# A gated cross-attention and ternary FFN layer: value products of 66 columns, square sums from bf16 parts, and another order of the steady slot

## The reference

```
h  = layernorm(x)
q  = rms_norm(h @ Wq + bq) * nq ;  k = rms_norm(ctx @ Wk + bk) * nk ;  v = ctx @ Wv + bv
a  = softmax(q k^T / sqrt(32)) v          16 heads of 32, within each tile of 128
x1 = x + tanh(g0) * (a @ Wo + bo)
u  = relu(layernorm(x1) @ T(Wfc))^2       T: ternary weights, hidden size 2048
out = x1 + tanh(g1) * rms_norm(u) @ T(Wproj)
```

## Time and profile before

| | us |
|---|---|
| median of 3 runs | 944.68 |
| lowest, highest | 942.75, 948.52 |
| span of the profiled execution | 945.4 |
| TensorE busy in it | 894.8 |
| ScalarE busy | 775.4 |
| VectorE busy | 715.2 |
| GpSimd busy | 572.2 |

### The profile page before, as it was taken

One profiled execution on the slowest core, in us unless ns is written; L12 is line 12 of the kernel. 1 busy time (PEld: TensorE's weight loads), 2 busy tenths in 40 slices (PEclk: granted clock), 3 DMA queues, 4 the chain that ended last, 5 costly groups with the idle time before them and its releaser, 6 DMA issues. The chain is left out here.

```text
span 945.4 us, 22870 instructions
## 1 busy us (share of the span) xinstructions
PE 894.8 (95%) x7958; PEld 535.9 (57%) x7958; DVE 715.2 (76%) x1448; ACT 775.4 (82%) x1559; POOL 572.2 (61%) x616
## 2 busy tenths in 40 slices
PE   5677798999999999999999999999999999999998
PEld 2333455466656656656656655556566656556664
DVE  6999999888877778878877778778777778776301
ACT  6888888888888888888888887888888888888673
POOL 1341436657676665657676665757676665757664
PEclk9797999999999999999999999999999999999999
DMA  9558874666666567666667665656765576755300
GB/s 360 141 96 206 201 157 79 113 112 124 120 128 118 110 121 124 123 118 119 120 127 127 100 122 112 122 115 126 121 135 112 105 128 117 127 91 97 68 24 34
DMA packets 319747, 115.80 MB, mean 122 GB/s; under 512 B 305168, under 2 KB 305168, under 8 KB 318096
## 3 DMA queue, kind: packets, MB, share of 16 engines
q1 hardware_dynamic: 319632, 114.34, 61.0%
HBM read 30.67 MB, written 8.39 MB: 41 GB/s over the span
## 5 line engine op out<-in xcount | busy, mean ns | idle before, releaser
L537 PE MATMUL up_pair<-ft,w 128*128 128x256 f16 x960 | 214.5, 273 | 0.2 <-DMA ft<-x_rows 0.2
L538 PE MATMUL up_pair<-ft,w 128*128 128x256 f16 x960 | 214.5, 273 | 0.0
L996 ACT ACTIVATE score_ps<-score_ps,exp_bias,exp_scale 128x128 f32<-128x128 f32 x512 | 189.9, 468 | 4.5 <-DVE exp_bias L1494 4.3
L2025 POOL TENSOR_TENSOR hh_sum<-hh_sum,hh_sb 128x512 f32<-128x512 f32 x112 | 159.1, 1421 | 49.5 <-ACT hh_sb L954 45.2
L552 PE MATMUL mix_ps<-w,big 128*128 128x512 bf16 x448 | 170.0, 380 | 0.7 <-DVE pt L1525 0.7
L553 PE MATMUL mix_ps<-w,big 128*128 128x512 bf16 x448 | 169.8, 379 | 0.0
L2015 POOL TENSOR_TENSOR big<-h_sb,big 128x512 f16<-128x512 f32 x128 | 149.4, 1167 | 25.1 <-POOL big L2015 9.1
L1970 POOL TENSOR_TENSOR ln_rstd<-ln_in,minus_half 128x1 f32<-128x1 f32 x64 | 36.9, 577 | 175.2 <-issue 145.2
L1327 DVE TENSOR_TENSOR p_rows<-score_ps,p_rows 128x512 f16<-128x512 f32 x128 | 85.5, 686 | 50.3 <-ACT p_rows L878 49.5
L878 ACT ACTIVATE p_rows<-score_ps 128x512 f16<-128x512 f32 x128 | 76.0, 639 | 40.1 <-DMA pt<-p_rows 39.8
L927 ACT ACTIVATE h_sb<-up_pair,relu_scale 128x512 f32<-128x512 f32 x120 | 81.7, 681 | 30.1 <-PE up_pair L538 29.8
(11 more groups left out here) (215 smaller groups left out, 2179.1 us busy)
## 6 DMA issues: line engine op xcount, KB each, us to landing
x_sb<-in_x SPq DMA_DIRECT2D x32, 256.0 KB, 3.1
ctx_sb<-in_ctx_t SPq DMA_DIRECT2D x32, 256.0 KB, 4.2
out<-out_sb SPq DMA_DIRECT2D x32, 256.0 KB, 2.3
big<-in_w_fc_t SPq DMA_DIRECT2D x4, 1024.0 KB, 5.3
big<-in_w_proj_t SPq DMA_DIRECT2D x4, 1024.0 KB, 5.9
pt<-p_rows SPq DMA_TRANSPOSE x128, 3.2
big<-in_wq_t SPq DMA_DIRECT2D x1, 1024.0 KB, 4.9
big<-in_wk_t SPq DMA_DIRECT2D x1, 1024.0 KB, 7.1
```

The source lines that it names most:

```text
L537: nc.tensor.matmul(dst[:, half], w, ft[i][:, c, :], start=(c == 0), stop=False)
L538: last = nc.tensor.matmul(dst[:, half], w, ft[i][:, C + c, :], start=False, stop=(c == C - 1))
L996: last = nc.scalar.activation(rows, rows, ACT.Exp, scale=exp_scale[:, :], bias=exp_bias[:, 4 * b + u:4 * b + u + 1])
L2025: nc.gpsimd.tensor_tensor(hh_sum[:, :], hh_sum[:, :], hh_sb[f % 2][:, :], ALU.add).then_inc(hsum_ready, 1)
```

## The change

1. *Values.* v_hi and v_lo of a head lie side by side in one tile, `v_both`. `wide_values` makes per head one 66-column product of p_hi with both, and one 33-column product of p_lo with v_hi: 32 products per slot in place of 48. The low part stands in columns of its own, so ScalarE copies it to SBUF (`values_low`, twice per slot), and VectorE's `wide_attention` adds it and then multiplies with the reciprocal, in place in SBUF. The results need four banks: b = 2 and 3 go to score banks 0 and 1, so `wide_values` waits there for k_raw and q_raw of the next tile, and the next `scores` for both halves of the attention.
2. *Square sums.* `hidden_split` on VectorE makes three bf16 parts of hh_sum (two copies, two subtractions, 128 x 256 each), and `square_sums_split` sums them with six bf16 products.
3. *Order.* The slots of all five queues are reordered. On SP, load_context moves from behind load_x to ahead of the last transpose of p, whose order becomes 0, 1, 2, 3, and the store goes to the end.

The first six slots and the closing slot keep their code, but for the shared tiles and one wait. The declarations of semaphores and of `ones_b`, and one memset, are left out here.

```diff
--- before.py
+++ after.py
@@ -63,14 +63,19 @@
             return [sem(f"{name}{i}") for i in range(n)]
 
 
-        score_ps = [stack.enter_context(nc.psum_tensor(f"score_ps{i}", [P, 512], F32)) for i in range(4)]
+        score_pair = stack.enter_context(nc.psum_tensor("score_pair", [P, 1024], F32))
+        score_ps = [score_pair[:, 0:512], score_pair[:, 512:1024]]
+        score_ps += [stack.enter_context(nc.psum_tensor(f"score_ps{i}", [P, 512], F32)) for i in (2, 3)]
         k_ps, q_ps, v_ps = score_ps[0:3]
         up_pair = stack.enter_context(nc.psum_tensor("up_pair", [P, 1024], F32))
         up_ps, up_b = up_pair[:, 0:512], up_pair[:, 512:1024]
-        mix_ps, tr_a = (stack.enter_context(nc.psum_tensor(n, [P, 512], F32)) for n in ("mix_ps", "tr_a"))
+        mix_pair = stack.enter_context(nc.psum_tensor("mix_pair", [P, 1024], F32))
+        mix_ps, tr_a = mix_pair[:, 0:512], mix_pair[:, 512:1024]
         o_ps = tr_a
         fc_ps = mix_ps[:, 512 - 8 * NU:512]
         pv_ps = [bank[:, 0:8 * (HD + 1)].rearrange("p (b u d) -> p b u d", b=2, d=HD + 1) for bank in (mix_ps, tr_a)]
+        wide_ps = [pair[:, :].rearrange("p (b k) -> p b k", b=2)[:, :, 0:8 * (HD + 1)].rearrange("p b (u c) -> p b u c", u=4)
+                   for pair in (mix_pair, score_pair)]
 
 
         ident = sb("ident", [P, P])
...
         warm_rows = w_hi[0][:, 0, 0:384]
-        v_hi = sb("v_hi", [P, H, HD + 1], F16)
-        v_lo = sb("v_lo", [P, H, HD + 1], F16)
+        v_both = sb("v_both", [P, H, 2 * (HD + 1)], F16)
+        v_hi, v_lo = v_both[:, :, 0:HD + 1], v_both[:, :, HD + 1:2 * (HD + 1)]
         p_inv = sb("p_inv", [P, H])
         p_rows = [sb(f"p_rows{i}", [P, 2, 512], F16) for i in range(PR)]
...
         t_scale = [out_sb[0][:, :].bitcast(BF16), sb("t_scale1", [P, 1024], BF16), out_sb[1][:, :].bitcast(BF16)]
+        pv_lo = t_scale[1][:, :].bitcast(F32).rearrange("p (i b u d) -> p i b u d", i=2, b=2, u=4)
+        hh_parts = abs_w[0][:, 0:3 * R].rearrange("p (n r) -> p n r", n=3)
         vb_wide = x1[0][:, :].rearrange("p (c k) -> p c k", c=C)
         ob_in = x1[1]
...
@@ -363,10 +373,11 @@
                 if t < NT:
                     transpose_p(t, 0)
                     transpose_p(t, 1)
+                    transpose_p(t, 2)
+                if t + 3 < NT:
+                    load_context(t + 3, (t + 3) % 2)
+                if t < NT:
                     transpose_p(t, 3)
-                    transpose_p(t, 2)
-                if s >= LAG:
-                    store(s - LAG, s % LAG)
                 if t + 1 < NT:
                     transpose_k(t + 1)
                     transpose_q(t + 1)
@@ -374,11 +385,12 @@
                     transpose_at(t)
                 if t + 3 < NT:
                     load_x(t + 3, (t + 3) % 4)
-                    load_context(t + 3, (t + 3) % 2)
                 if t + 2 < NT:
                     transpose_x(t + 2)
                 if s >= 0 and t >= 3:
                     transpose_x1(s)
+                if s >= LAG:
+                    store(s - LAG, s % LAG)
 
             load_x(0, 0)
...
 
+            def square_sums_split(t):
+
+                if t == 2:
+                    pe.wait_ge(ones_b_ready, 1)
+                pe.wait_ge(hpart_ready[3], t // 2)
+                pe.wait_ge(relu_ready, UP * (t + 2))
+                for i in range(2):
+                    for n in range(3):
+                        last = nc.tensor.matmul(up_ps[:, i:i + 1], hh_parts[:, n, i * P:(i + 1) * P], ones_b[:, 0:1],
+                                                start=(n == 0), stop=(n == 2))
+                    last.then_inc(hss_done, 1)
...
                 need(pe, plo_ready, 4 * t)
+                need(pe, attn_ready, 2 * t)
                 for u in range(4):
                     col = slice(u * P, (u + 1) * P)
                     for n, (q, k) in enumerate(((qt_hi, kt_hi), (qt_hi, kt_lo), (qt_lo, kt_hi))):
@@ -625,6 +650,24 @@
                         last = nc.tensor.matmul(dst, pt[b][:, 1, q], v_hi[:, h, :], start=False, stop=True)
                     last.then_inc(pv_done, 1)
 
+            def wide_values(t):
+
+                need(pe, x1_ready, t)
+                need(pe, out_ready, t - LAG)
+                for b in range(4):
+                    pe.wait_ge(pt_in[b], 16 * t + 16)
+                    if b == 2:
+                        pe.wait_ge(kraw_ready, t + 2)
+                    if b == 3:
+                        pe.wait_ge(qraw_ready, t + 2)
+                    for u in range(4):
+                        h = 4 * u + b
+                        q = slice(u * P, (u + 1) * P)
+                        dst = wide_ps[b // 2][:, b % 2, u, :]
+                        nc.tensor.matmul(dst, pt[b][:, 0, q], v_both[:, h, :], start=True, stop=False)
+                        last = nc.tensor.matmul(dst[:, 0:HD + 1], pt[b][:, 1, q], v_hi[:, h, :], start=False, stop=True)
+                    last.then_inc(pv_done, 1)
+
             def project_out(t):
...
@@ -696,24 +739,24 @@
                 scores(t)
                 ffn_down(s - LAG, range(4, 12), mix_ps)
                 project_out(s)
+                ffn_up(g, j, 0, up_b)
                 ffn_down(s - LAG, range(12, 15), mix_ps)
-                ffn_up(g, j, 0, up_b)
-                if s % 2 == 0:
-                    square_sums(s - LAG)
-                ffn_down(s - LAG, range(15, 16), mix_ps)
                 if more:
                     next_keys(t)
+                ffn_down(s - LAG, range(15, 16), mix_ps)
+                if s % 2 == 0:
+                    square_sums_split(s - LAG)
+                if more:
                     next_queries(t)
                     ffn_up(g, j, 1, up_ps)
+                    next_values(t)
+                wide_values(t)
                 ffn_up(g, j, 2, up_b)
-                values(t)
                 if more:
-                    next_values(t)
+                    ffn_up(g, j, 3, up_ps)
                 if t + 2 < NT:
                     next_context(t)
                 ffn_down(s + 1 - LAG, range(0, 4 if more else 16), mix_ps)
-                if more:
-                    ffn_up(g, j, 3, up_ps)
 
...
 
+            def values_low(t, i):
+                act.wait_ge(pv_done, 4 * t + 2 * i + 2)
+                if t == 6:
+                    act.wait_ge(tern_ready, NU)
+                need(act, attn_sum, 2 * (t - 6))
+                nc.scalar.activation(pv_lo[:, i], wide_ps[i][:, :, :, HD + 1:2 * HD + 1], ACT.Copy).then_inc(pv_lo_ready, 1)
+
             def slot(t):
                 s = t - 1
                 g, j = s // J, s % J
                 more = not last_slot(t)
-                halves((s - 1) // J, (s - 1) % J, 3)
-                squares((s - 1) // J, (s - 1) % J, 3)
                 if more:
                     context_hi(t + 1, (t + 1) % 2)
+                halves((s - 1) // J, (s - 1) % J, 3)
                 exps(t, 0)
+                probs_hi(t, 0)
                 exps(t, 1)
-                probs_hi(t, 0)
+                probs_hi(t, 1)
+                squares((s - 1) // J, (s - 1) % J, 3)
                 exps(t, 2)
-                probs_hi(t, 1)
                 probs_hi(t, 2)
+                relu(g, j, 0, up_b)
                 exps(t, 3)
-                probs_hi(t, 3)
-                relu(g, j, 0, up_b)
-                if t + 2 < NT:
-                    x_hi(t + 2)
                 halves(g, j, 0)
                 squares(g, j, 0)
                 if more:
                     key_squares(t + 1)
-                    query_squares(t + 1)
+                probs_hi(t, 3)
+                if t + 2 < NT:
+                    x_hi(t + 2)
                 relu(g, j, 1, up_ps)
                 if more:
+                    query_squares(t + 1)
                     k_hi(t + 1)
                     q_hi(t + 1)
-                normed_hi(s)
+                values_low(t, 0)
+                values_low(t, 1)
                 halves(g, j, 1)
-                relu(g, j, 2, up_b)
-                attention_hi(t)
                 if more:
                     v_hi_of(t + 1)
+                normed_hi(s)
+                attention_hi(t)
+                squares(g, j, 1)
+                relu(g, j, 2, up_b)
                 halves(g, j, 2)
-                squares(g, j, 1)
                 relu(g, j, 3, up_ps)
                 squares(g, j, 2)
...
 
+            def hidden_split(t):
+
+                if t == 2:
+                    dve.wait_ge(tern_ready, NU)
+                dve.wait_ge(hsum_ready, 2 * UP * (t // 2 + 1))
+                need(dve, hss_done, t if t > 2 else 0)
+                nc.vector.tensor_copy(hh_parts[:, 0, :], hh_sum[:, 0:R]).then_inc(hpart_ready[0], 1)
+                dve.wait_ge(hpart_ready[0], t // 2)
+                nc.vector.tensor_tensor(hh_sum[:, 0:R], hh_sum[:, 0:R], hh_parts[:, 0, :],
+                                        ALU.subtract).then_inc(hpart_ready[1], 1)
```

(57 more changed lines are left out.)

5 lines of the change are left out of this document (added).

## The result

The changed kernel has a median of 934.55 us (934.22 to 939.36) against 944.84 for the kernel before in the same runs: a ratio of 0.9901, 95% interval 0.9880 to 0.9921. The forecast was 934.9. The profiled span is 933.6 us.

The account below looks back on a forecast made before the run. TensorE, busy 95% of the span, was taken as the bound: 945.4 span - 8.2 (value products) - 2.6 (square sums) + 1.0 (bad landings) = 935.6, less 0.7 from span to median: 934.9 us. Range 931 to 946.

Parts of the forecast that it names:

- 1.0 for bad landings: Estimated us added to the span for transposes that land late at the last probabilities, ft and the q transpose.
- Wide products: TensorE's value products per slot: 0.88 us instead of 1.21, 0.33 less, 8.2 us over 25 slots.
- Square sums: Six bf16 products on TensorE, 0.15 us instead of 0.37, in 12 slots: 2.6 us less.
- Rival 3: Wide products don't gain: 60 ns each, 0.15 us lost per slot, 946 us; chance 0.05.
- (a): Tail of the slot: v_lo ready at 25.65 us, scores need it at 26.15; slack 0.5, against 0.9 before.
- (b): Last probabilities: their transpose lands at 19.2 us, at worst 20.9, before wide_values; slack 1.4, worst stall 0.3.
- (c): ft, the transpose up 0 needs: lands at 6.3 us; slack 0.5, stall up to 1.8 in 12 slots.
- (d): Square sums' inputs: hidden_split done at 11.6 us, TensorE asks at 12.90; covered by 1.3.
- (e): The q transpose on SP: issued at 21.7 us, landing by 24.9, at worst 26.6, needed at 26.15.
- (f): project_out's transpose: leaves at 25.1 us, lands at 28.3, needed at 30.4.
- Rival 1: Late transposes: 0.1 to 0.4 us of stall per slot, giving 937 to 945 us; chance 0.25.
- Rival 2: Late tail: GpSimd blocks VectorE instructions with two SBUF inputs; one block 949 us, two 976; chance 0.10.

Follow-up runs that it names:

- c_order: The changed kernel with the old value products, old attention and fp32 square sums, so that only the new order is left; 944.09 us, ratio 0.9998.
- c_narrow: The changed kernel with the old 48 value products of 33 columns and the old attention; 941.85 us, ratio 0.9973.
- c_fp32: The changed kernel with the old fp32 square sums; 937.69 us, ratio 0.9933.
- o_pool: o_wide with GpSimd's slot alone in its new order; 974.95 us, ratio 1.0317.
- sp_old: The changed kernel with SP's queue alone in its old order; 943.03 us, ratio 0.9977.
- a_ctx: The changed kernel with load_context behind the q transpose instead of ahead of the last p transpose; 933.27 us, ratio 0.9872.
- b_gap: The changed kernel with GpSimd's rows_plus_constant moved right behind x1_norm; 936.67 us, ratio 0.9907.
- o_wide: The kernel before, in its old order on all queues, with the wide products and their attention put in; 964.22 us, ratio 1.0211.
- o_psum: o_wide with the attention sum kept in PSUM, so no mult has two inputs in SBUF; 943.36 us, ratio 0.9980.
- p_three: The changed kernel with three idle VectorE reads per steady slot between x_lo and attention_lo; 968.18 us, ratio 1.0243.

## Why the prediction was right, point by point

- *TensorE is the bound, all else is cover*: right. c_order and c_narrow stand within 0.3 us of the kernel before less the work taken out of TensorE; c_fp32 and the changed kernel within 0.5 us if the 1.0 for bad landings is added to theirs, and 1.5 and 0.5 us above their sums without it.
- *Wide products*: 0.88 us forecast, 0.89 measured. The pair of 66 and 33 columns takes 56 ns (16 of them 0.89 us), 55 forecast. With 25.2 for the narrow one the wide one takes 30. *Square sums*: 0.15 forecast and measured. Rival 3 is out.
- *The new order's times*: value products forecast at 19.98 us in the slot, found at 19.97; square sums 12.90 and 12.90; relu 1 17.6 and 17.59; attention_hi's end 24.3 and 24.14; v_lo's end 25.65 and 25.54. The periods 26.07 and 26.22 were found as 26.08 and 26.23.
- *(a)*: the walk was right, the slack wrong: 0.5 was forecast; the distance is 0.69, of which 0.36 pass from v_lo's end to the scores' start, so 0.33 are left. The prediction put this passage at nothing, and the added wait on attn_ready with it. GpSimd's x1_norm was put at 22.3 and ends at 22.05, 0.13 us behind the start of the first mult and not in front of it. That mult takes its 0.42 and ends 0.29 to 0.30 us behind x1_norm in all 25 slots, which is where a held mult ends: it stands at the very edge. In o_pool, where x1_norm ends 0.05 us later against the mult (523.38 and 523.20), the mult takes 0.45.
- *(b)*: probs_hi 3 at 14.5 was found at 14.44, but the issue of the last p transpose, forecast at 15.95, is found at 16.86 in that slot (500.91), since SP was still at the one before and then issued load_context (500.25). So the walk is wrong in this place: slack was 1.4 on paper, and with a landing after 3.28 us it is 0.5 (504.19, read at 504.69). Where the landing took 5.0 and 5.2 us (issued at 236.64 and 394.79) TensorE waited 0.4 and 0.6. sp_old and a_ctx show the same transpose as the one that the order of the DMAs moves most.
- *(c)*: ft was issued at 2.0, forecast 2.5; its waits are 0.2 us.
- *(d)*: hidden_split forecast from 9.95 to 11.6 and found from 9.93 to 11.47; no wait.
- *(e), (f)*: k and q were put at 20.4 and 21.7 and leave at 20.31 and 21.63; one of them, at 772.8 us, lets the scores wait 0.8, the largest wait of the steady slots. (f) was put at 25.1 and leaves at 24.96; no steady slot waits for it.
- *The sum*: 10.8 less 1.0 was forecast for the steady slots and 10.0 was found, 10.8 less 0.8. So the mechanism holds, and not the number alone. The step from the span to the median doesn't: each execution on record has a time 1.7 to 1.9 us above its own span (935.51 and 933.6 for the profiled one), so the time is not quite that from the first to the last instruction, and the 0.7 set the median of several executions against the span of another, slower one (945.4, a time near 947). It does no harm, since the forecast is in effect the median before less 9.8 us (944.68 to 934.9), and the medians differ by 10.3. That the 1.0 added for landings came so near is in part luck: the delays of the steady slots, 2.2 us before, add up to 3.0 in the changed kernel, but to 1.1 in a_ctx and 3.2 in b_gap.
- *Rival 1* (0.25) did not come: the delays of the DMAs are 3.0 us in all, 0.8 more than before, where it needed 0.1 to 0.4 in every slot.
- *Rival 2* was given 0.10 and did not come. The same mechanism costs 21 us in the old order (o_wide against o_psum). What kept it away is a gap in GpSimd's queue of 2.7 us, which only the walk through the new order gives. b_gap shows that even one block of 0.49 us in this gap costs next to nothing (656.9 us for the steady slots in place of 656.7), since VectorE is idle 0.36 us ahead of attention_lo; the price of 25 times a block less the slack leaves this idle time out.

## What to carry to other kernels

Where one engine is busy all the time, price an edit by the start-to-start distances of that engine, and then walk every other queue through the new order to see what comes due when; here that gave the places named above to within 0.35 us on the four compute engines, but missed one DMA's issue by 0.9, because SP was busy with the one before. An edit that saves work on the bound and adds some elsewhere can lose more than it saves in the unchanged order (o_wide: +20 us), and one operand moved from SBUF to PSUM can give nearly all of that back. Count the waits that stand behind the one that ends last, too (0.11 us for one record more at the scores). Reorder queues together: GpSimd's queue alone in the new order (o_pool) made the kernel slower, and SP's alone left in the old one (sp_old) took away most of the gain. Which of the moves in the queues of TensorE, ScalarE and VectorE are needed is open; no run takes them one by one.

## What the runs showed of the hardware that I had not expected

A VectorE product with two SBUF inputs waits for the end of a GpSimd instruction that started before it (0.91 us in b_gap, up to 1.49 in o_wide, for 0.42), and one that started 0.10 us before the GpSimd sum is not slowed (b_gap); with one input in PSUM it was 424 to 426 ns in all 50 cases of o_psum, GpSimd running beside each. What is held ends a fixed time behind the GpSimd instruction: 0.28 to 0.29 us for 256 columns (o_wide, b_gap), 0.55 for 512 (attention_lo in o_wide, o_psum, p_three). So of the 0.42 us of a free mult the first 0.13 can overlap the GpSimd instruction at no cost.

From the end of the record of a VectorE instruction to the start of the matmul that waits for it there were 0.06 us at next_context (o_wide), 0.25 at the scores with one further record of waits behind (before) and 0.36 with two (p_three). This is to be taken off any slack that is read between two rows.
